# Row maxima over three PSUM banks: one VectorE instruction per tile in place of four, from the second batch on

## The reference

```
x = x + xattn(layernorm(x), ctx)        # softmax(q k^T / 8) v, then Wo
x = x + ffn(layernorm(x))               # soft dispatch and combine over 2048 slots
```

## Time and profile before

| what | us |
|---|---|
| median of 3 runs | 436.92 (436.57 to 438.42) |
| the profiled execution | 434.98 |
| its span in the trace | 433.1 |
| TensorE busy | 422.2 (97%) |
| VectorE busy | 333.9 (77%) |
| ScalarE busy | 245.8 (57%) |
| GpSimd busy | 165.1 (38%) |

### The profile page before, as it was taken

The page is one execution under the profiler, slowest core; times in us unless marked ns, Lnnn a source line. Parts: engine busy times, 40 slices in busy tenths (PEclk is TensorE's granted clock), DMA queues, the critical chain, the costliest instruction groups (busy, mean ns, idle before and its releaser), DMA issues.

```text
span 433.1 us, 7463 instructions
## 1 busy us (share of the span) xinstructions
PE 422.2 (97%) x3002; PEld 386.6 (89%) x3002; DVE 333.9 (77%) x613; ACT 245.8 (57%) x413; POOL 165.1 (38%) x95
## 2 busy tenths in 40 slices
PE   7899999999999999999999999999999999999897
PEld 4798999999999999889999998899999898999887
DVE  3688747876786768767898689978988899679981
ACT  3477646665565446645663766556655564644641
POOL 2509900515050305031708044617146543456720
PEclk9999999999999999999999999999999999999999
DMA  8311020114011011100120001001000000296000
GB/s 225 82 53 14 6 85 14 42 45 113 14 37 49 20 12 17 70 18 14 13 73 20 12 14 71 21 12 15 0 20 13 1 14 18 49 247 192 2 2 23
DMA packets 15028, 19.05 MB, mean 44 GB/s; under 512 B 3997, under 2 KB 10925, under 8 KB 14994
## 3 DMA queue, kind: packets, MB, share of 16 engines
q1 hardware_dynamic: 14994, 18.58, 16.9%
HBM read 18.32 MB, written 0.26 MB: 43 GB/s over the span
## 4 chain that ended last, share of the span: by engine, by line
PE 73%; DVE 11%; ACT 5%; DMA 5%; POOL 5%; issue 1%; SPq 1%; POOLq 0%; ACTq 0%
PE turned L722 14%; PE scores L706 7%; PE acc L742 7%; PE acc L744 7%; PE acc L743 7%; PE scores L712 7%; PE scores L709 7%; PE misc L759 3%; DVE pT_l L1399 2%; DVE small L1389 2%; PE misc L626 2%; ACT prob L1144 2%; DMA ctx_raw<-in_ctx_dram 2%; DMA rden_row<-small 2%; PE scores L1074 2%; PE misc L786 2%
## 5 line engine op out<-in xcount | busy, mean ns | idle before, releaser
L1137 ACT CAST pT_h<-turned 125x512 fp32r<-125x512 f32 x168 | 95.3, 591 | 123.8 <-PE turned L722 123.2
L1399 DVE TENSOR_TENSOR pT_l<-turned,pT_h 125x512 fp32r<-125x512 f32 x168 | 112.3, 686 | 60.3 <-ACT pT_h L1137 59.3
L1389 DVE TENSOR_REDUCE small<-scores 128x1 f32<-128x500 f32 x168 | 107.9, 672 | 5.5 <-PE scores L712 5.2
L722 PE MATMUL turned<-ident,prob 128*125 128x128 f32 x672 | 94.7, 276 | 2.1 <-DVE pT_l L1399 1.9
L722 PEld LDWEIGHTS turned<-ident,prob 128*125 128x125 f32 x672 | 87.5, 187 | 10.0 <-DVE pT_l L1399 4.0
L742 PE MATMUL acc<-pT_h,ctx_nh 125*128 125x256 f32 (+1 forms) x288 | 94.2, 327 | 0.0
L1144 ACT ACTIVATE prob<-scores,small 128x1500 f32<-128x1500 f32 x56 | 85.0, 1518 | 11.1 <-DVE small L1392 10.6
L744 PE MATMUL acc<-pT_h,ctx_nl 125*128 125x256 f32 (+1 forms) x288 | 86.4, 300 | 0.0
L743 PE MATMUL acc<-pT_l,ctx_nh 125*128 125x256 f32 (+1 forms) x288 | 86.3, 300 | 0.0
L706 PE MATMUL scores<-ctx_th,qk_h 128*128 128x500 f32 x168 | 67.6, 403 | 1.3 <-ACT prob L1144 1.3
L712 PE MATMUL scores<-ctx_th,qk_l 128*128 128x500 f32 x168 | 65.3, 389 | 0.0
(11 more groups left out here) (207 smaller groups left out, 560.4 us busy)
## 6 DMA issues: line engine op xcount, KB each, us to landing
ctx_raw<-in_ctx_dram SPq DMA_DIRECT2D x7, 750.0 KB
rbc<-rden_row SPq DMA_DIRECT2D x15, 128.0 KB, 3.5
rbc<-rden_row SPq DMA_DIRECT2D x8, 192.0 KB, 3.0
eb<-in_L_ffn_expert_b_dram SPq DMA_DIRECT2D x4, 256.0 KB, 5.7
wq_sb<-in_L_xattn_Wq_dram SPq DMA_DIRECT2D x1, 512.0 KB, 3.8
wk_sb<-in_L_xattn_Wk_dram SPq DMA_DIRECT2D x1, 512.0 KB, 6.8
wv_sb<-in_L_xattn_Wv_dram SPq DMA_DIRECT2D x1, 512.0 KB, 9.2
wo_sb<-in_L_xattn_Wo_dram SPq DMA_DIRECT2D x1, 512.0 KB, 9.8
```

Of the source, the lines that this page charges most:

```text
L722: last = tr(turned[0:CK, m, 128 * c:128 * c + 128], prob[u][:, CK * j:CK * j + CK], ident[:, :])
L1137: nc.scalar.copy(pT_h[0:CK, PLACES[g // NT % 2][t], CPB * k:CPB * k + CPB, :], turned[0:CK, (KB * u + k) % 2, :].rearrange("p (c r) -> p c ...
L1389: m = v.tensor_reduce(bankmax[:, u, k:k + 1], scores[:, k, 0:KW], AX.X, ALU.max)
L1399: v.tensor_tensor(pT_l[0:CK, place, dst, :], turned[0:CK, (KB * u + k) % 2, :].rearrange("p (c r) -> p c r", c=CPB), pT_h[0:CK, place, dst ...
```

## The change

```diff
@@ row_max(g, u) on VectorE
             def row_max(g, u):
 
+                if g >= NT:
+                    dve.wait_ge(scores_pe, KB * (g + 1))
+                    v.tensor_reduce(negmax[:, u:u + 1], scores[:, :, 0:KW], AX.XY, ALU.max,
+                                    negate=True).then_inc(negmax_dve, 1)
+                    return
                 for k in range(KB):
                     dve.wait_ge(scores_pe, KB * g + (k + 1))
                     m = v.tensor_reduce(bankmax[:, u, k:k + 1], scores[:, k, 0:KW], AX.X, ALU.max)
```

## The result

| what | before | changed |
|---|---|---|
| median of four runs, us | 437.21 | 447.89 (447.48 to 449.44) |
| the profiled execution, us | 434.98 | 448.25 |
| its span, us | 433.1 | 446.3 |
| TensorE busy, us | 422.2 | 427.6 |
| VectorE busy, us | 333.9 | 314.6 |

The account below looks back on a forecast made before the run. TensorE, busy in 422.2 of 433.1 us, was taken as the bound. Terms 8.4 + 0.2 + 1.3 + 0.5 + 0.5 + 0.3 = 11.2 us on the median 436.92 gave 448.1 us, range 442.5 to 453.5.

Parts of the forecast that it names:

- D: Duration of the wide reduction on VectorE, 1.70 us; as a rival: maxima not on TensorE's path, within the 0.06 for absorbed.
- Readiness at E + 1.74: In (4,3), batch 4 row tile 3, the maximum is ready 1.74 us after the last score matmul, 0.83 later than before.
- E: Moment the tile's last score matmul ends; as a rival: TensorE's clock falls in stretches, 5 to 15 us more, chance 0.03.
- Tiles t = 3, 4, 5 of batches 2 to 6: 15 row tiles where the third transposes follow `pT_l` closely: each pays 0.57 us, one 0.46, 8.4 us in all.
- t = 1, 2: 0.2; t = 0, 6: nothing: Other row tiles of batches 2 to 6: t = 1, 2 lose 0.2 us together; t = 0, 6 have time to spare.
- Batch 1: TensorE also waits for ScalarE's copy behind the exponential: (1,4) +0.83, (1,3) and (1,5) +0.4 each, sum with (1,1) 1.3 us.
- (1,1), -0.34: Batch 1, row tile 1: VectorE comes late, held by a DMA, so the shorter single instruction gains 0.34 us.
- Where VectorE was late: Tiles whose maxima start late, after a string now 0.83 us later: (5,1) +0.5, (7,1) +0.5, (7,4) and (7,5) together +0.3.
- TensorE's wait for `pT_l`: Sign in the new profile: TensorE's wait for this VectorE result rises from 5.9 to about 15 us in some 30 places.
- VectorE 23 us less busy: Over the 49 changed tiles, VectorE is busy 0.47 us less per tile, 23 us in all, beside TensorE's work.
- Rival A: VectorE's freed time counts: gains where VectorE begins after the last score matmul, 435.5 us, at most 431.0; chance of faster 0.03.
- C: Rival, the wide view is dear: reduction of 2.9 us gives 495 us, of 2.02 us gives 458; together 0.08.

Follow-up runs that it names:

- late tiles only: Kernel before, with one wide reduction only in (5,1), (7,1), (7,2), (7,5) and (7,6): 435.25 us, ratio 0.9977 to the kernel before.
- the last one: Kernel before, with the wide reduction only in five late tiles and third transposes behind the last chunk in t = 3, 4, 5 of batches 2 to 6: 432.52 us.
- the experiment on the third transposes: Changed kernel with the third group of transposes moved behind the last chunk of context products: 443.58 us, ratio 1.018 to the kernel before.

## Why the prediction was right

It said 448.1 us and 11.2 us more than before; the median was 447.89, 10.7 more, and the loop of the trace 11.7 more. By its own steps:

- *D.* 1.70 was taken from the slope of contiguous reductions; the group shows 1720 ns. The two jumps between banks are cheap: the group lies 0.02 us above an estimate that has nothing for them. (The Trainium skill, "VectorE: DVE Perf Modes", in the section on the TRN2 errata, prices a VectorE operation from PSUM at 120 cycles and one per element at 0.96 GHz; the estimate by these figures for 1500 elements is 1.69 us, and the trace agrees within 2%.)
- *Readiness at E + 1.74 and `pT_l` at E + 2.35, transposes at E + 2.40*: 1.76, 2.36 and 2.41.
- *Tiles t = 3, 4, 5 of batches 2 to 6, 8.4 us*: 8.6; each 0.56 to 0.59. The 0.16 between `pT_l` and the transposes, and the 0.46 that one tile was to pay for it, are not in the trace of before: there it is 0.05 in all 15. These tiles are the bulk of the loss: the experiment with them alone took 8.0 us more than before.
- *t = 1, 2: 0.2; t = 0, 6: nothing*: 0.1 and 0.0. Shown by the experiment with t = 0 and 6 alone too.
- *Batch 1*: (1,3), (1,4) and (1,5) took 0.39, 0.83 and 0.37 more (0.4, 0.83, 0.4 forecast). In (1,4) the load for the next head now waits for ScalarE's copy, which the earlier trace rows had shown with nothing to spare:

```profile
90.37 0.43 ACT L1130 COPY ahead<-misc 128x336 f32<-128x336 f32 x1
```

```profile
90.85 0.19 PEld L640 LDWEIGHTS misc<-xa_h,wqk_h 128*128 128x128 f32 x1 [0.51 <-ACT ahead L1130]
```

- *(1,1), -0.34*: this term failed in the comparison of the two traces, +0.02. VectorE's reduction is shorter there as forecast: from its start to the next tile's first score matmul 4.30 us pass, before 4.63. But VectorE was let go later by its DMA, 1.09 us after E and before 0.73. SyncE issues the write of `rden_row` at 53.01 us and the read of it, which waits for the write to land, at 61.34 before; in the changed kernel they are at 54.54 and 63.45:

```profile
54.54 0.32 SPq L389 DMA_DIRECT2D rden_row<-small  x1
63.45 0.32 SPq L392 DMA_DIRECT2D rbc<-rden_row  x1
```

That is 8.3 us from issue to issue before, 8.9 now. It is not the change: in the five experiments whose code up to there is that of the kernel before (t = 3, 4, 5 only, t = 0 and 6 only, (5,0) and (7,0) only, late tiles only, and the last one), (1,1) took 8.00 to 8.44 us against 7.55 in the profile of before, with the same 4.61 to 4.63 us behind VectorE's start. The forecast was worked out on one profile with an early landing; up to 0.9 us of the loop differs between profiled executions for this reason alone. That the sum met the median within 0.5 us is therefore partly luck.
- *Where VectorE was late: (5,1) +0.5, (7,1) +0.5, (7,4) and (7,5) together +0.3*: +0.51, +0.51, and +0.70 - 0.38 = +0.32. (The 0.72 of (7,4) does not follow from 0.17 to spare, which leaves 0.66. The next scores start no sooner than 0.05 or 0.06 behind the accumulator's end, in the changed kernel's (7,4) as in the tile (4,3) of the experiment on the third transposes, so that 0.12 were to spare.) The experiment on (5,0) and (7,0) showed that the loss of these tiles comes from the tile ahead (+0.82 and +0.84) and the one on (5,1) and (7,1) that the instruction itself gives 0.33 back there; 0.83 - 0.33 is the 0.5. The maxima of (5,1) in the changed kernel, VectorE:

```profile
253.04 0.67 DVE L1429 TENSOR_TENSOR oT<-acc,rbc 128x384 f32<-128x384 f32 x1
253.62 1.72 DVE L1389 TENSOR_REDUCE small<-scores 128x1 f32<-128x1500 f32 x1
```

- *TensorE's wait for `pT_l`*: "about 15 us in some 30 places" was written, 24.1 in 46 came. This sign was missed. The profile books one stall both on the weight load and on the matmul, as in (4,3), where the matmul has 0.47:

```profile
221.40 0.51 PEld L722 LDWEIGHTS turned<-ident,prob 128*125 128x125 f32 x4 [0.68 <-DVE pT_l L1404]
```

The 5.9 from which the forecast started was such a double sum too; the loads alone went from 4.0 in 8 places to 15.3 in 27.
- *VectorE 23 us less busy*: 19.3 (333.9 to 314.6). The forecast added up single durations, but instructions back to back overlap: the 168 reductions of 0.672 make 112.9 us by that sum and 107.9 busy. Neither number enters the forecast of the time.
- *Rival A* (the freed time of VectorE counts) holds in tiles where VectorE starts after E and TensorE waits for what follows, and nowhere else. In (7,2) VectorE starts 0.86 us after E, the wide instruction ends sooner, and the tile takes what it took, since `pT_l` had 0.6 us to spare. Over the whole kernel VectorE was 19 us less busy and the kernel 10.7 us slower. The rule of the Trainium skill named there ("VectorE: DVE Perf Modes", "Rules for kernel authors"), to minimise the count of chained VectorE operations, agrees with the trace in those tiles only. *C* fell with the 1720 ns, *D* with every experiment. *E* did not occur in the loop of the profiled execution; the 3.4 us at 0.50 lie ahead of it. The earlier trace rows show batch 5 alone; the changed kernel was granted 1.00 over this longer stretch too, and so was the kernel before:

```profile
103.00:400.00 297.00, 287.86 (x1908) 262.05 (x1907) 216.57 (x279) 167.52 (x267) 105.74 (x43) 1.00 0.15 32
```

## What to carry to other kernels

A reduction split along the order in which its input is produced hides all but its last piece; merged, it saves its fixed parts and shows its whole length behind the last input. So ask, place by place, when the engine would be free: merging can pay where it comes after the last input (0.3 us a tile here), and splitting pays where it stands ready before. And follow the result to whoever waits in order: the same 0.85 us cost 0.57 in one tile, nothing in another, and 0.83 one tile further on in a third.

## What was not expected of the hardware

In batch 1 the small write of `rden_row` (1.5 KB) is issued 0.33 us after the 750 KB load of a context. The next DMA, which waits for it to land, was issued 8.33 us later in one execution and 9.07 in another of the same code up to there, while the median of the 23 such writes from issue to landing is 3.0 us. In the kernel before no other of them is issued less than 8 us behind a load. That the load holds the write is therefore likely, but no run moved the one away from the other. In (1,1) TensorE waits for it.
